# Linear attention of layer 0 rebuilt on one core: one stream of 16 slots, padded heads, sums of squares on TensorE

## The chip, the cores and the metric

The kernel runs on one core of a Trainium2 chip. Its engines are TensorE (PE, with its weight loads shown apart as PEld), VectorE (DVE), ScalarE (ACT), GpSimd (POOL) and SyncE (SP), which issues the DMAs. Metric is the device time of one execution in microseconds (us), median over runs.

## What is computed

Two transformer layers over x of 4 sequences x 512 tokens x 256 features, all float32. The change lies in the first of four parts, a linear attention with 16 heads of 16 features, of which this is the core (the code works in blocks of 128 tokens, which gives the same sums):

```python
qkvu = layernorm(x) @ W_qkvu.T            # q, k, v, u of 256 features each
q, k = silu(q), silu(k)                   # per head, decay s = slope_rate[head]
for block in blocks:                      # kv: the 16x16 state of a head
    o  = (q * exp(-s*i)) @ kv + ((q @ k.T) * exp(-s*(i-j)) [i>=j]) @ v
    kv = exp(-s*len) * kv + (k * exp(-s*(len-i))).T @ v
o = o * rsqrt(mean(o*o, -1) + 1e-6)       # over all 256 features
x = x + (u * o) @ W_out.T
```

The parts behind it (a gated feed-forward layer with Hadamard-transformed weights, a narrow attention, a wide causal attention, a mixture of experts) are untouched in what they compute.

## The kernel before

One program holds a hand-written instruction list for each engine; semaphores order them. Tokens are cut into 16 tiles of 128, four (t) to a sequence (b). Float32 products run as two passes, so one `matmul` is two MATMUL and two LDWEIGHTS records in the trace; a transpose is one of each.

**Start.** SP loads the weights, and TensorE turns them in 12 groups (`START`, lines 514 to 523; `turn_weights`, line 1392), DVE emptying the even groups (line 761) and ACT the odd ones (line 1136). Between its groups ACT makes the decay tables with 16 exponentials (line 1142), which DVE masks (line 764) before it stages the first sequence (line 773). POOL meanwhile runs the butterflies of the feed-forward weights `wugd` (lines 600 and 601) and scales them (lines 610 and 614); its end is the semaphore `fw_done`.

**Linear attention** is a loop over the four sequences in which nothing of one sequence overlaps the next. TensorE: 8 transposes of the normalised x (line 1412), which ACT empties (line 1155); q and k with features on partitions, 8 products of 512 columns (line 1423, emptied by ACT with Silu, line 1167); then per tile k and v in one product pair (line 1431) and u (line 1435), with tokens on partitions, emptied by ACT (lines 1173 and 1174) and DVE (line 784). DVE multiplies q by its decay (line 775), masks k into two copies, even and odd heads (line 781), and multiplies each tile's k by its decay (line 786). Per tile then: the scores of 16 heads, each with 32x128 weights (line 1446), into banks 0 to 3; DVE multiplies them by the decay table (line 796, four per tile); the values: for each head the 128x128 decayed scores are the weights and 16 columns of v move (line 1473), 16 products per tile; the product with the state (line 1479); the new state k.T @ v (line 1461), which DVE masks (line 811) and folds in (line 820). DVE multiplies the output by u (line 805), ACT squares and sums it from the bank (line 1178). When the four tiles are done, `ou` is turned (line 1485), emptied (line 1182) and multiplied by W_out (line 1490, 8 products of 256 columns), and ACT copies the result to `y0` (line 1185).

**After the loop** come, one behind the other: the root of the mean squares (lines 828 and 1188), the residual on all 16 tiles (line 833), the feed-forward weights turned in 16 groups (`FFN`, line 1399, emptied on lines 840 and 1193), the layer norm of all 16 tiles (lines 717, 720, 737), the staging copy (line 845), and TensorE's first transpose of the feed-forward layer (line 1412). Its products are on lines 1509 and 1517. SP waits for `rms_in` (line 556) before it loads the wide attention's weights.

Of the kernel before, what the change touches and what calls it, by code (L numbers as in the profile page):

```python
# [5 lines left out]
ALU = mybir.AluOpType  # L6
# [6 lines left out]
P = 128  # L13
D = 256
# [60 lines left out]
def two_layers(nc, x_in, slope, W_qkvu, W_out0, SU_ug, SU_dp, Wscale_ug, Wscale_dp, W_up, W_gate, W_down,  # L75
               Wq1, Wk1, Wv1, Wo1, ln_w, ff_ln_w, wq, wk, wv, wo, wg, w1, w3, w2, consts, out):
    ctx = ExitStack()
    with ctx:
# [72 lines left out]
        wqkvuT = first.enter_context(nc.sbuf_tensor("wqkvuT", [P, DC, 4 * D], F32))  # L151
        wout0T = first.enter_context(nc.sbuf_tensor("wout0T", [P, DC, D], F32))
# [8 lines left out]
        qT = early.take(DC, S)  # L161
        qdT = early.take(DC, S)
        kT = early.take(DC, S)
        kTm = early.take(2, DC, S)
        ks = early.take(2, D)
        kd = early.take(TB, D)
        v0 = early.take(TB, D)
        u0 = early.take(TB, D)
        PT0 = late.take(2, H16, P)
        kvs = early.take(DC, P)  # L170
        kvt = ks[:, 1, :].rearrange("p (c e) -> p c e", c=DC)
        ou = early.take(TB, D)
        osq = ks[:, 0, :]
        ouT = kT
        ss = early.take(NT)
        y0 = xn

        def head_of(slot):
# [5 lines left out]
        l0 = {n: sem("l0_" + n) for n in ("stage", "xT_ps", "xT_sb", "qk_ps", "q_sb", "kv_ps", "k_sb", "v_sb", "u_ps",  # L184
                                          "u_sb", "kTm", "kd", "s_ps", "pt", "o_ps", "st_ps", "st", "ou", "sq",
                                          "ouT_ps", "ouT_sb", "y_ps", "y_sb", "chain", "qd")}
# [326 lines left out]

        def start_turns():
            for c in range(DC):
                for blocks, dst in ((range(0, 4), wqkvuT[:, c, 0:512]), (range(4, 8), wqkvuT[:, c, 512:1024]),
                                    (range(8, 10), wout0T[:, c, :]), (range(10, 13), wqkv1T[:, c, :])):
                    yield wnat, c, list(blocks), dst
            for i in range(4):
                yield wo_nat, 0, [i, 4 + i], wo1p[:, i, :]  # L520

        wo_nat = xn_st[:].rearrange("p t d -> p (t d)").rearrange("p (n q) -> p n q", q=P)
# [4 lines left out]
        FFN += [(wugd, k % 2, [16 + k // 2, 20 + k // 2], wdT[:, k, :], su_dp[:, k:k + 1]) for k in range(IC)]  # L527


        @block.sync  # L530
        def _(sync):
# [24 lines left out]
            sync.wait_ge(rms_in, 1)  # L556
# [154 lines left out]

        def dve_norm(v, phase, eps, src=x, dst=xn, rms=False):
# [17 lines left out]
            v.wait_ge(ln_std, phase + 1)  # L730
# [11 lines left out]
        def _(v):  # L742
            dve_norm(v, 0, 1e-5)
# [7 lines left out]
            vch.inc(nc.vector.memset(wo_nat, 0.0))  # L751
            vch.wait(v)
            for blk in range(DC):
                ins = nc.vector.tensor_copy(
                    wo_nat[:, 4 * blk:4 * blk + 4, :].rearrange("p i (g d) -> p i g d", d=32)[:, :, :, 0:HD16],
                    wnat[:, 13 + blk, :].rearrange("p (g i d) -> p i g d", g=KV16, d=HD16))
            ins.then_inc(wo_spread, 1)
            for n, (_src, c, blocks, dst) in enumerate(START):
                if n % 2 == 0:
                    v.wait_ge(wt_ps, n + 1)  # L760
                    nc.vector.tensor_copy(dst, bank[n % 8][:, 0:P * len(blocks)]).then_inc(wt_sb[0], 1)
# [5 lines left out]
            v.wait_ge(wt_ps, len(START))  # L767

            ch = Count(l0["chain"], 2)
            with v.Fori(0, B) as b:  # L770
                ch.n = 0
                v.wait_ge(l0["xT_ps"], b * DC + 1)
                nc.vector.tensor_copy(xn_st[:], xn[:, bass.ts(b, TB), :]).then_inc(l0["stage"], 1)
                v.wait_ge(l0["q_sb"], b * 4 + 2)
                nc.vector.tensor_tensor(qdT.rearrange("p c (t i) -> p c t i", t=TB),
                                        qT.rearrange("p c (t i) -> p c t i", t=TB),
                                        QD.unsqueeze(2).to_broadcast([P, DC, TB, P]), ALU.mult).then_inc(l0["qd"], 1)
                v.wait_ge(l0["q_sb"], b * 4 + 4)
                par = const("parity")
                for e in range(2):  # L780
                    nc.vector.tensor_scalar(kTm[:, e, :, :], kT, par[:, e:e + 1], None, ALU.mult).then_inc(l0["kTm"], 1)
                for t in range(TB):
                    v.wait_ge(l0["u_ps"], b * TB + t + 1)
                    nc.vector.tensor_copy(u0[:, t, :], bank[(7, 1)[t % 2]][:, 0:D]).then_inc(l0["u_sb"], 1)
                    v.wait_ge(l0["k_sb"], b * TB + t + 1)
                    nc.vector.tensor_tensor(kd[:, t, :].rearrange("p (h d) -> p h d", h=H16),
                                            ks[:, t % 2, :].rearrange("p (h d) -> p h d", h=H16),
                                            KD.unsqueeze(2).to_broadcast([P, H16, HD16]),
                                            ALU.mult).then_inc(l0["kd"], 1)

                def decay(t):
                    for g in range(4):
                        v.wait_ge(l0["s_ps"], b * 16 + 4 * t + g + 1)
                        if g == 0 and t >= 2:
                            v.wait_ge(l0["o_ps"], b * TB + t - 1)
                        nc.vector.tensor_tensor(PT0[:, t % 2, 4 * g:4 * g + 4, :],
                                                bank[g][:].rearrange("p (h i) -> p h i", h=4),
                                                DT[:, 4 * g:4 * g + 4, :], ALU.mult).then_inc(l0["pt"], 1)

                decay(0)  # L800
                for t in range(TB):
                    if t + 1 < TB:
                        decay(t + 1)
                    v.wait_ge(l0["o_ps"], b * TB + t + 1)
                    nc.vector.tensor_tensor(ou[:, t, :], bank[4 + t % 2][:, 0:D], u0[:, t, :],
                                            ALU.mult).then_inc(l0["ou"], 1)
                    if t < TB - 1:
                        v.wait_ge(l0["st_ps"], b * 3 + t + 1)
                        into = kvs if t == 0 else kvt
                        a, _b = mid("block")  # L810
                        kv_ins = nc.vector.tensor_tensor(into[:], bank[6][:, 0:D].rearrange("p (c e) -> p c e", c=DC),
                                                         con[:, None, a:_b].to_broadcast([P, DC, P]), ALU.mult)
                        if t == 0:
                            kv_ins.then_inc(l0["st"], 1)
                        else:
                            ch.inc(kv_ins)
# [309 lines left out]
        def _(act):  # L1126
# [36 lines left out]
            with act.Fori(0, B) as b:  # L1163
# [4 lines left out]
                for t in range(TB):  # L1168
                    act.wait_ge(l0["kv_ps"], b * TB + t + 1)
                    if t >= 2:  # L1170
                        act.wait_ge(l0["kd"], b * TB + t - 1)
# [676 lines left out]
```

## Time and profile before

| | us |
|---|---|
| median of 3 runs | 2391.54 (2389.66 to 2395.81) |
| the profiled execution | 2396.13 |
| its span | 2394.2 |
| linear attention, first transpose to last output copy | 40.9 to 350.4 |
| from there to the first transpose of the feed-forward layer | 350.4 to 376.9 |
| mean granted TensorE clock of the span | 0.906 of 2.4 GHz |

How to read it: an engine's busy time adds the durations of its instructions; a matmul's duration overlaps that of its neighbours, so the pace of a row of matmuls is the distance of their starts. The granted clock is 1.00 at 2.4 GHz and 0.50 at 1.2 GHz. In the timeline a row merges instructions of one line that follow each other: start, time from the first start to the last end, count, and in brackets how long the engine was idle before and what released it.

### The profile page before, as it was taken

How to read it: one execution, taken by the hardware profiler on the slowest of the kernel's cores; microseconds unless marked ns; L12 is line 12 of the kernel's file. 1: busy time of each engine (PE TensorE's matmuls, PEld its weight loads, DVE VectorE, ACT ScalarE, POOL GpSimd, SP SyncE). 2: the span in 40 equal slices, each digit the busy share in tenths (PEclk: the TensorE clock that was granted, in tenths of full speed). 3: DMA queues.
4: the chain of work that ended last, by engine and by line, in shares of the span. 5: the costliest groups of instructions: out<-in, count | busy, mean ns of one | idle time of the engine just before them, and what ended most of it. 6: DMA issues, size and time to landing. Idle time of an engine off the chain costs nothing.

```text
span 2394.2 us, 36552 instructions
## 1 busy us (share of the span) xinstructions
PE 2030.8 (85%) x10710; PEld 1287.3 (54%) x10710; DVE 1255.0 (52%) x3206; ACT 1041.2 (43%) x2677; POOL 905.6 (38%) x1013
## 2 busy tenths in 40 slices
PE   3889987996687775599999999999999997689995
PEld 2767774554333332366666666666666664555553
DVE  5542233114576675666666666666666666632222
ACT  3012211111454553366565556656565664234442
POOL 4970000000121200244444444444444444268885
PEclk8577668998699998799999999999999999599998
DMA  4000010000000101000000000000000000835556
GB/s 133 1 0 0 0 33 20 0 0 0 0 1 1 36 1 38 1 1 0 0 0 0 0 0 0 0 0 0 0 0 0 0 0 1 283 55 82 83 84 156
DMA packets 61330, 60.47 MB, mean 25 GB/s; under 512 B 13136, under 2 KB 58320, under 8 KB 61264
## 3 DMA queue, kind: packets, MB, share of 16 engines
q0 software_dynamic: 15360, 20.98, 5.5%
q1 hardware_dynamic: 45904, 38.65, 5.0%
q8 instruction: 36, 0.59, 0.1%
q14 instruction: 30, 0.25, 0.0%
HBM read 40.48 MB, written 19.14 MB: 25 GB/s over the span
## 4 chain that ended last, share of the span: by engine, by line
PE 64%; DVE 12%; issue 10%; ACT 7%; POOL 3%; DMA 1%; SPq 1%; ACTq 0%; DVEq 0%; POOLq 0%
PE banks L1549 7%; PE banks L1572 7%; PE banks L1581 6%; PE banks L1509 5%; PE banks L1560 5%; PE banks L1473 4%; PE banks L1591 4%; PE banks L1771 2%; PE banks L1645 2%; PE banks L1517 2%; PE banks L1603 2%; ACT wide_x L1271 2%; PE banks L1620 2%; POOL wdT L692 2%; ACT wugT L1285 2%
## 5 line engine op out<-in xcount | busy, mean ns | idle before, releaser
L900 DVE TENSOR_REDUCE con<-banks 128x1 f32<-128x256 f32 (+3 forms) x512 | 250.0, 488 | 147.7 <-PE banks L1551 141.0
L1549 PE MATMUL banks<-wide_k,wide_q 128*128 128x512 f32 (+3 forms) x1024 | 300.5, 376 | 0.5 <-ACT wide_k L1222 0.5
L624 POOL TENSOR_TENSOR wugT<-wugT,con 128x512 f32<-128x512 f32 (+1 forms) x256 | 237.6, 934 | 134.9 <-DVE con L890 134.3
L1549 PEld LDWEIGHTS banks<-wide_k,wide_q 128*128 128x128 f32 x1024 | 159.3, 190 | 132.3 <-issue 86.2
L1572 PE MATMUL banks<-attn 128*64 128x256 f32 x1280 | 208.5, 404 | 1.0 <-ACT attn L1250 1.0
L1591 PE MATMUL banks<-late,xnT 128*128 (+1 forms) x512 | 197.2, 508 | 9.8 <-DVE xn L916 6.3
L932 DVE TENSOR_REDUCE con<-banks 128x2 f32<-128x1024 f32 x128 | 154.7, 1214 | 68.0 <-PE banks L1633 67.0
L635 POOL TENSOR_TENSOR attn<-attn 128x320 f32<-128x320 f32 x128 | 110.9, 866 | 200.2 <-DVE attn L878 200.2
L1235 ACT ACTIVATE wugT<-banks,con 128x512 f32<-128x512 f32 (+1 forms) x256 | 161.1, 631 | 58.3 <-DVE con L900 55.0
L1581 PE MATMUL banks<-late,attn 128*128 (+1 forms) x512 | 141.7, 399 | 28.0 <-DVE attn L883 25.8
L1771 PE MATMUL banks<-w,late 128*128 x320 | 156.1, 610 | 2.6 <-issue 1.6
L643 POOL MEMSET narrow_x<- 128x2560 f32 x1 | 2.2, 2231 | 399.3 <-DVE x L853 399.3
L922 DVE TENSOR_TENSOR wide_x<-attn,wide_x 128x256 fp32r<-128x256 f32 (+1 forms) x256 | 110.8, 473 | 61.6 <-ACT wide_x L1271 61.6
L706 POOL DMA_INDIRECT y_rows<-xnT,scatter_at x80 | 127.0, 1587 | 34.4 <-issue 22.2
L1560 PE MATMUL banks<-con,wugT 128*128 128x128 f32 x896 | 136.8, 275 | 0.0
L1112 DVE TENSOR_TENSOR late<-late,banks 128x256 f32<-128x256 f32 x80 | 33.7, 421 | 195.5 <-ACT late L1377 168.0
L1250 ACT ACTIVATE attn<-banks 128x512 f32<-128x512 f32 x160 | 95.3, 596 | 92.0 <-PE banks L1560 90.2
L1603 PE MATMUL banks<-ident_r,wide_x 128*128 128x128 f32 x768 | 112.1, 256 | 25.6 <-DVE wide_x L922 22.0
L911 DVE COPY attn<-banks 128x512 f32<-128x512 f32 x160 | 110.0, 688 | 38.4 <-PE banks L1560 38.3
L624 POOL TENSOR_TENSOR wdT<-wdT,con 128x256 f32<-128x256 f32 x128 | 78.4, 613 | 124.5 <-DVE con L890 121.3
L1551 PE MATMUL banks<-causal,ident_h 128*128 128x128 bf16 x512 | 118.1, 231 | 0.0
L1509 PE MATMUL banks<-xnT,wugT 128*128 128x512 f32 x256 | 115.6, 614 | 2.9 <-ACT xnT L1155 2.9
(276 smaller groups left out, 4118.1 us busy)
## 6 DMA issues: line engine op xcount, KB each, us to landing
w<-in_L_ffn_w_dram SPq DMA_DIRECT2D x32, 256.0 KB, 6.3
late<-in_L_ffn_w_dram SPq DMA_DIRECT2D x16, 256.0 KB, 6.4
y_rows<-wqkv1T SPq DMA_DIRECT2D x1, 2176.0 KB, 7.9
x<-in_L_attn_x_dram SPq DMA_DIRECT2D x4, 512.0 KB, 8.8
late<-in_L_ffn_wq_dram SPq DMA_DIRECT2D x2, 1024.0 KB, 7.3
late<-in_L_ffn_wo_dram SPq DMA_DIRECT2D x1, 2048.0 KB, 9.7
h_rows<-wugT SPq DMA_DIRECT2D x1, 2048.0 KB, 7.6
y_rows<-x SPq DMA_DIRECT2D x1, 2048.0 KB, 13.8
```

The source lines that it names most:

```text
L624: nc.gpsimd.tensor_tensor(p, p, rinv[:, m:m + 1].to_broadcast([P, n]), ALU.mult).then_inc(at.sem["norm"], 1)
L900: nc.vector.tensor_reduce(negmax[:, a:a + 1], bank[at.sbank(a)][:, 0:P * at.keys(at.row_of(a))], AX, ALU.max, negate=True).then_inc(at.sem ...
L932: nc.vector.tensor_reduce(n_max[:, s % 4, j // 4, j % 4, :], banks[1 + pair % 2][:].rearrange("p (e n) -> p e n", e=2), AX, ALU.max, negat ...
L1235: nc.scalar.activation(at.prob(m)[:, 0:n], bank[at.sbank(m)][:, 0:n], ACT.Exp, bias=negmax[:, m:m + 1], accum_out=rowsum[:, m:m + 1]).then ...
L1509: ins = nc.tensor.matmul(bank[2 + 2 * (k % 2) + j][:], wugT[:, c, INTER * j + P * k:INTER * j + P * k + P], xnT[:, c, :], start=(c == 0), ...
L1549: nc.tensor.matmul(sbank[:, 0:keys], wide_q[:, side, i, qcols], wide_k[:, side, w, 0:keys], start=(w == 0), stop=False)
L1560: ins = nc.tensor.transpose(bank[PTBANK[a % 2]][:, P * i:P * i + P], at.prob(4 * q + i)[:, P * k:P * k + P], ident)
L1572: ins = nc.tensor.matmul(bank[OBANK][HD64 * e:HD64 * e + HD64, 0:D], wide_v[:, side, k, :], pT.rearrange("p (c e n) -> p e c n", e=2, n=P) ...
L1581: ins = nc.tensor.matmul(bank[YBANK][:, 0:D], at.onT[:, a % ring, P * c:P * c + P], w_out(n, c), start=(c == 0), stop=(c == chunks - 1))
L1591: ins = nc.tensor.matmul(bank[YBANK][:, 0:QKV], xnT[:, c, P * a:P * a + P], w_qkv(n, c), start=(c == 0), stop=(c == DC - 1))
L1603: ins = nc.tensor.transpose(bank[MBANK][:, P * h:P * h + P].bitcast(F32R), src[:, t % 2, z + P * h:z + P * h + P], ident_r[:])
L1771: ins = nc.tensor.matmul(bank[j % 2], m_xT[:, j % 2, c, :], w13[:, bass.ds(e, 1), c, :, :].rearrange("p e i d -> p (e i d)"), start=(c == ...
```

## The change

The four sequences become one unrolled stream of 16 slots, one for each tile (`LIN`). Slot s of each engine holds that tile's values, gate, state and squares, the scores of tile s+1 and the output product of tile s-1. Into three places of each slot (`beside`) the projections of the next sequence are dealt out (`LIN_NEXT`), in the last sequence the 16 groups of feed-forward weights (`FFN`, kinds "w"). These side products and the outputs y share banks 5 and 6 in turn; scores keep banks 0 to 3, the values have bank 4 alone, the new state bank 7.

- The values change sides: v, padded from 16 to 32 features per head, is the weights (128x32) and the 128 columns of decayed scores move, four heads at a time to the four groups of 32 partitions of one bank. The output has features on partitions (4 groups of 128, half of them zeros), so `ou` needs no transposes, and the products with the state are four of 128 columns instead of two.
- u comes with features on partitions too, padded: 4 x 2 products of 512 columns a sequence (`wuS`) for 4 x 2 of 256. W_out is padded likewise (`wout0S`): 4 products of 256 columns a tile for 2.
- The mean square: ACT squares the whole bank into `osq`, and four products with a column of ones as the moving operand sum it into column 256 of the bank of y. ACT copies y and that column.
- k's two masked copies are written by ACT (Silu with the mask as scale) instead of DVE. The staging copy `xn_st` of each sequence goes; x is transposed from `xn`.
- The root, residual, statistics and layer norm run per sequence inside the next sequence's slots (`mean_square`, `residual`, `normalised` on DVE; `rms_root`, `norm_root` on ACT); for the last sequence behind slot 15. SP's wait for `rms_in` becomes one for all four.
- At the start, 16 groups are turned instead of 12 (38 transposes for 34), DVE clears and fills the padded places.

```diff
-        wqkvuT = first.enter_context(nc.sbuf_tensor("wqkvuT", [P, DC, 4 * D], F32))
-        wout0T = first.enter_context(nc.sbuf_tensor("wout0T", [P, DC, D], F32))
+        wqkvT = first.enter_context(nc.sbuf_tensor("wqkvT", [P, DC, 3 * D], F32))
+        wuS = first.enter_context(nc.sbuf_tensor("wuS", [P, DC, H16, 32], F32))
+        wout0S = first.enter_context(nc.sbuf_tensor("wout0S", [P, 4, D], F32))
...
+        turned_bufs = [Region(wugT[:].rearrange("p c n -> p (c n)")), early]
+        qT = [r.take(DC, S) for r in turned_bufs]
+        qdT = [r.take(DC, S) for r in turned_bufs]
+        uT = [r.take(4, S) for r in turned_bufs]
+        kTm = [Region(wdT[:].rearrange("p k d -> p (k d)")).take(2, DC, S), early.take(2, DC, S)]
         ks = early.take(2, D)
+        ou = early.take(2, 4, P)
+        osq = early.take(2, 4, P)
...
+        LIN_FIRST = [("x", 0), ("x", 1), ("q", 0), ("q", 1), ("k", 0), ("k", 1), ("kv", 0), ("u", 0), ("u", 1), ("u", 2), ("u", 3),
+                     ("kv", 1), ("kv", 2), ("kv", 3)]
+        LIN_NEXT = (((("x", 0), ("x", 1)), (("q", 0),), (("q", 1),)), ((("k", 0),), (("k", 1),), (("kv", 0),)),
+                    ((("u", 0),), (("u", 1),), (("kv", 1),)), ((("u", 2),), (("u", 3),), (("kv", 2), ("kv", 3))))
+        LIN = B * TB
+        LIN_BANKS, LIN_O, LIN_STATE = (5, 6), 4, 7
+        def beside(slot, place):
+            b, t = divmod(slot, TB)
+            if b + 1 < B:
+                return [(kind, b + 1, i) for kind, i in LIN_NEXT[t][place]]
+            return [("w", 0, 4 * t + i) for i in ((0,), (1,), (2, 3))[place]]
...
+            sync.wait_ge(rms_in, B)
...
+            vch.inc(nc.vector.memset(wo_nat, 0.0))
+            vch.inc(nc.vector.memset(wo0_nat, 0.0))
+            vch.inc(nc.vector.memset(wuS[:], 0.0))
...
+            nc.vector.memset(v0, 0.0)
+            nc.vector.memset(kvs, 0.0).then_inc(wo_spread, 1)
...
+            def gated(s):
+                b, t = divmod(s, TB)
+                v.wait_ge(l0["o_ps"], s + 1)
+                v.wait_ge(l0["u_sb"], 4 * b + 4)
+                if s >= 2:
+                    v.wait_ge(l0["y_ps"], s - 1)
+                nc.vector.tensor_tensor(ou[:, s % 2], bank[LIN_O].rearrange("p (r i) -> p r i", r=4),
+                                        uT[b % 2][:, :, P * t:P * t + P], ALU.mult).then_inc(l0["ou"], 1)
...
+                else:
+                    vch.inc(nc.vector.tensor_tensor(kvt.rearrange("p (c m) d -> p c (m d)", c=DC), ps, mask, ALU.mult))
+                    vch.wait(v)
+                    v.wait_ge(l0["o_ps"], s + 1)
+                    for c in range(DC):
+                        old = kvs[:, 8 * c:8 * c + 8, 0:HD16]
+                        ins = nc.vector.scalar_tensor_tensor(old, old, BD[:, c:c + 1], kvt[:, 8 * c:8 * c + 8, :], ALU.mult, ALU.add)
+                    ins.then_inc(l0["st"], 1)
...
+            decay(0)
+            decayed_q(0)
+            for t in range(TB):
+                decayed_k(0, t)
+            for s in range(LIN):
+                b, t = divmod(s, TB)
+                if s + 1 < LIN:
+                    decay(s + 1)
+                gated(s)
+                if t < TB - 1:
+                    state(s)
+                for part in range(3):
+                    for kind, n, i in beside(s, part):
+                        if kind == "kv":
+                            decayed_k(n, i)
+                        elif kind == "w" and i % 2 == 0:
...
+                if t == 1 and b + 1 < B:
+                    decayed_q(b + 1)
+                if b >= 1 and t >= 1:
+                    (mean_square, residual, normalised)[t - 1](b - 1)
+            for phase in (mean_square, residual, normalised):
...
+                nc.scalar.activation(osq[:, s % 2].rearrange("p r i -> p (r i)"), bank[LIN_O], ACT.Square).then_inc(l0["sq"], 1)
+            def lin_out(s):
+                at = bank[lin_bank("y", 0, s)]
+                act.wait_ge(l0["y_ps"], s + 1)
+                nc.scalar.activation(y0[:, s, :], at[:, 0:D], ACT.Copy)
+                nc.scalar.activation(ss[:, s:s + 1], at[:, D:D + 1], ACT.Copy).then_inc(l0["y_sb"], 1)
...
+            def lin_values(s):
+                b, t = divmod(s, TB)
+                o = bank[LIN_O]
+                if s >= 1:
+                    pe.wait_ge(l0["ou"], s)
+                    pe.wait_ge(l0["sq"], s)
+                if t >= 1:
+                    pe.wait_ge(l0["st"], 3 * b + t)
+                    pe.wait_ge(l0["qd"], b + 1)
                     for r in range(4):
+                        nc.tensor.matmul(o[:, P * r:P * r + P], kvs[:, 4 * r:4 * r + 4, :].rearrange("p g d -> p (g d)"),
+                                         qdT[b % 2][:, r // 2, P * t:P * t + P], start=(r == 0), stop=False, skip_group_check=True)
+                pe.wait_ge(l0["v_sb"], TB * b + t + 1)
+                for r in range(4):
+                    for g in range(4):
+                        if r == 0:
+                            pe.wait_ge(l0["pt"], 4 * s + g + 1)
+                        ins = nc.tensor.matmul(o[32 * g:32 * g + 32, P * r:P * r + P], v0[:, t, 4 * r + g, :],
+                                               PT0[:, s % 2, 4 * g + r, :], start=(t == 0 and r == 0), stop=(r == 3),
+                                               skip_group_check=True)
+                ins.then_inc(l0["o_ps"], 1)
+            def new_state(s):
+                b, t = divmod(s, TB)
+                pe.wait_ge(l0["kd"], TB * b + t + 1)
+                if s >= 1:
+                    pe.wait_ge(l0["st"], 3 * b + t)
                 for c in range(DC):
+                    ins = nc.tensor.matmul(bank[LIN_STATE][:, P * c:P * c + P], kd[:, t, P * c:P * c + P],
+                                           v0[:, t, 8 * c:8 * c + 8, 0:HD16], start=True, stop=True)
+                ins.then_inc(l0["st_ps"], 1)
+            def lin_out(s):
+                n = lin_bank("y", 0, s)
+                at = empty(n)
+                pe.wait_ge(l0["sq"], s + 1)
+                for r in range(4):
+                    nc.tensor.matmul(at[:, D:D + 1], osq[:, s % 2, r, :], const("ramp")[:, 0:1], start=(r == 0), stop=(r == 3))
+                for r in range(4):
+                    ins = nc.tensor.matmul(at[:, 0:D], ou[:, s % 2, r, :], wout0S[:, r, :], start=(r == 0), stop=(r == 3))
+                ins.then_inc(l0["y_ps"], 1)
+                emptied[n] = l0["y_sb"], s + 1
+            early_uses, late_uses = LIN_FIRST[:6], LIN_FIRST[6:]
+            lin_side([(kind, 0, i) for kind, i in early_uses])
+            scores(0)
+            lin_side([(kind, 0, i) for kind, i in late_uses])
+            for s in range(LIN):
+                if s + 1 < LIN:
+                    scores(s + 1)
+                lin_side(beside(s, 0))
+                lin_values(s)
+                lin_side(beside(s, 1))
+                if s % TB < TB - 1:
+                    new_state(s)
+                if s >= 1:
+                    lin_out(s - 1)
+                lin_side(beside(s, 2))
+            lin_out(LIN - 1)
```

## Rows read from the trace of the kernel before

**Rows 1.** The page: engine totals, and TensorE's clock in 40 slices of the span.

```profile
PE 2030.8 (85%) x10710; PEld 1287.3 (54%) x10710; DVE 1255.0 (52%) x3206; ACT 1041.2 (43%) x2677; POOL 905.6 (38%) x1013
...
PEclk8577668998699998799999999999999999599998
```

**Rows 2.** Windows: PE, PEld, DVE, ACT, POOL busy, clock, DMA share, GB/s.

```profile
40.90:125.70 84.80, 71.80 (x360) 57.31 (x360) 41.51 (x39) 11.85 (x27) 83.39 (x37) 0.64 0.00 1
...
203.80:278.60 74.80, 68.16 (x360) 55.00 (x360) 20.24 (x39) 12.84 (x28) 0.00 (x0) 0.68 0.00 0
278.60:350.40 71.80, 64.95 (x361) 51.88 (x361) 19.54 (x38) 13.04 (x30) 0.00 (x0) 0.71 0.00 0
350.40:376.90 26.50, 7.39 (x49) 6.76 (x49) 24.02 (x77) 7.43 (x12) 0.00 (x0) 0.65 0.48 119
```

**Rows 3.** Windows of 4 us, PE alone: busy (matmuls), granted clock, DMA.

```profile
60.00:64.00 4.00, 4.00 (x14) 1.00 0.02 4
76.00:80.00 4.00, 4.00 (x20) 0.50 0.00 0
600.00:604.00 4.00, 2.53 (x9) 0.50 0.00 0
692.00:696.00 4.00, 3.02 (x28) 1.00 0.00 0
```

**Rows 4.** Timeline of PE, third sequence of the linear attention.

```profile
206.13 7.13 PE L1423 MATMUL banks<-xnT,wqkvuT 128*128 128x512 f32 x16 [1.23 <-ACT xnT L1155]
...
214.82 1.03 PE L1435 MATMUL banks<-wqkvuT,xnT 128*128 128x256 f32 x4
...
224.19 1.17 PE L1446 MATMUL banks<-early 32*128 32x128 f32 x32 [0.61 <-DVE early L784]
225.30 0.71 PE L1461 MATMUL banks<-early 128*128 128x128 f32 x4
226.10 3.11 PE L1446 MATMUL banks<-early 32*128 32x128 f32 x32
...
252.99 7.01 PE L1473 MATMUL banks<-early,late 128*128 128x16 f32 x32
```

**Rows 5.** Timeline of PE in the narrow attention, values with 128x32 weights.

```profile
691.60 1.06 PE L1645 MATMUL banks<-wugT,attn 128*32 128x512 f32 x8
692.60 0.54 PE L1654 MATMUL banks<-ident_r,narrow_mx 128*128 128x128 f32 x4
```

**Rows 6.** Timeline of all engines, behind the last sequence.

```profile
350.38 3.71 PE L1399 MATMUL banks<-con,early 128*128 128x128 f32 x32 [0.78 <-ACT xn L1185]
...
352.18 6.43 DVE L833 SCALAR_TENSOR_TENSOR x<-xn,rstd,x 128x256 f32<-128x256 f32 x16
...
363.13 5.31 DVE L717 BATCH_NORM_STATS2 st<-x 128x6 f32<-128x256 f32 x16
...
376.88 1.97 PE L1412 MATMUL banks<-con,xn_st 128*128 128x128 f32 x8 [13.75 <-DVE xn_st L845]
```

**Rows 7.** Timeline of all engines, start of the first sequence.

```profile
34.60 0.63 ACT L1136 ACTIVATE wo1p<-banks 128x256 f32<-128x256 f32 x2
34.72 3.85 DVE L764 TENSOR_TENSOR late<-late,con 128x2048 f32<-128x2048 f32 x1 [6.31 <-ACT early L1147]
...
40.92 1.33 PE L1412 MATMUL banks<-con,xn_st 128*128 128x128 f32 x5 [12.75 <-DVE xn_st L773]
43.58 9.24 PE L1423 MATMUL banks<-xnT,wqkvuT 128*128 128x512 f32 x16 [0.69 <-ACT xnT L1155]
```

**Rows 8.** Lines of DVE: ns min/median/max, first and last start; POOL's last work.

```profile
L786 DVE TENSOR_TENSOR early<-early x16: 416/1324/2233, 59.0 to 298.9; 128x256 f32<-128x256 f32 x16
L796 DVE TENSOR_TENSOR late<-banks,late x64: 675/681/693, 68.6 to 329.7; 128x512 f32<-128x512 f32 x64
L820 DVE SCALAR_TENSOR_TENSOR early<-early x16: 344/352/2475, 93.1 to 334.0; 128x128 f32<-128x128 f32 x16
166.64 2.33 POOL L614 TENSOR_SCALAR early<-early,ws_dp 128x1024 f32<-128x1024 f32 x2
```

More of the change, by code:

```diff
@@ L764, in _ @@
             vch.inc(nc.vector.tensor_tensor(DT, DT, con[:, None, a:_b].to_broadcast([P, H16, P]), ALU.mult))
-            vch.wait(v)
[L767 to L776, printed above, removed]
-                                        QD.unsqueeze(2).to_broadcast([P, DC, TB, P]), ALU.mult).then_inc(l0["qd"], 1)
[L778 to L816, printed above, removed]
-                            ch.wait(v, b)
-                            v.wait_ge(l0["st"], b * 5 + 2 * t - 1)
-                            for c in range(DC):
-                                nc.vector.scalar_tensor_tensor(kvs[:, c, :], kvs[:, c, :], BD[:, c:c + 1], kvt[:, c, :],
-                                                               ALU.mult, ALU.add).then_inc(l0["st"], 1)
@@ new lines, in normalised @@
+            def normalised(b):
+                rows = slice(TB * b, TB * b + TB)
+                v.wait_ge(ln_std, b + 2)
+                vch.inc(nc.vector.reciprocal(rstd[:, rows], std[:, rows]))
+                vch.wait(v)
+                for t in range(TB * b, TB * b + TB):
+                    nc.vector.tensor_scalar(xn[:, t, :], x[:, t, :], mv[:, t, 0:1], rstd[:, t:t + 1],
+                                            ALU.subtract, ALU.mult).then_inc(xn_all, 1)
+            decay(0)
+            decayed_q(0)
@@ L1133, in start_weights @@
                 for n in turns:
[L1134 removed]
+                    _src, _c, _blocks, copies = START[n]
                     act.wait_ge(wt_ps, n + 1)
[L1136 removed]
+                    for dst, part in copies:
+                        ins = nc.scalar.activation(dst, part(bank[n % 8]), ACT.Copy)
+                    ins.then_inc(wt_sb[1], 1)
             start_weights(range(1, 9, 2))
@@ new lines, in scores @@
+            def scores(s):
+                b, t = divmod(s, TB)
+                cols = slice(P * t, P * t + P)
+                pe.wait_ge(l0["q_sb"], 2 * b + 2)
+                pe.wait_ge(l0["k_sb"], 2 * b + 2)
+                for r in range(4):
+                    for g in range(4):
+                        if r == 0 and s >= 1:
+                            pe.wait_ge(l0["pt"], 4 * (s - 1) + g + 1)
+                        rows = slice(32 * g, 32 * g + 32)
+                        ins = nc.tensor.matmul(bank[g][:, P * r:P * r + P], kTm[b % 2][rows, r % 2, r // 2, cols],
+                                               qT[b % 2][rows, r // 2, cols], start=True, stop=True)
+                        if r == 3:
+                            ins.then_inc(l0["s_ps"], 1)
```

364 lines of the change are left out of this document (201 added, 163 removed).

## The prediction

> **What bounds the kernel now.** I read the page first: TensorE is busy for 85% of the span, and its clock in the second to sixth of the 40 slices (60 to 360 us) is 5, 7, 7, 6 and 6 tenths, the longest low run there is [rows 1]. The change touches only what lies before the feed-forward layer, so I cut that stretch with the windows view: the linear attention takes 309.5 us (40.9 to 350.4), and 26.5 us of norms and weight turning follow before TensorE's next stage [rows 2]. In the sequences TensorE is busy 85 to 91% of the time, DVE 27 to 49%, ACT 14 to 18%. So TensorE bounds it, but at a mean clock of 0.64 to 0.71. The 4 us windows say where the clock goes: while projections run it is granted 1.00, while the values run (line 1473) 0.50, with the engine shown busy all the time in both [rows 3]. The timeline of one sequence gives the reason to suspect: the values are 32 passes of only 16 moving columns, 7.01 us a tile, 0.22 us a pass, and that is the load of 128 weight columns, not the product [rows 4]. Four of them a sequence are 28 us of some 75, and they leave the clock low for the transposes and the first half of the output product behind them. Behind the last sequence TensorE works 7.4 of 26.5 us while DVE walks through 16 tiles three times [rows 2, 6].
>
> **The change, part by part.** I sum TensorE's work of one sequence at full clock, since a bound engine sets the end, and add waits afterwards. A product is two passes.
> - Projections: q and k 16 passes of 512 columns, u 16 (8 of them new, from the padding), k with v 16: 48 passes. Sixteen took 7.13 us [rows 4], 0.44 each with the last one's tail taken off: 21.1 us. Eight transposes at 3.71 / 32 = 0.116 [rows 6]: 0.9.
> - Scores, unchanged: 32 passes in 1.17 us at full clock [rows 4], four times: 4.7.
> - Values, new form: 32 passes of 128 columns with 128x32 weights. No row has this shape. Lower bound: eight passes of 512 columns with 128x32 weights in the narrow attention start at 691.60 and the next line at 692.60, 1.00 us for 4096 columns, and ours are 32 x 128, also 4096 [rows 5]. Upper bound: no overlap between the four column groups, a quarter of 0.44 per pass, 3.5 us. I take 1.17, the scores' price: the same count, the same 128 columns, the same four-way split. Four tiles: 4.7, where 28 were.
> - State: 3 tiles of 8 passes of 128 columns at 0.116: 2.8. New state: four passes take 0.80 us until the next line starts (225.30 to 226.10) [rows 4], three times: 2.4.
> - Output: 8 passes of 256 columns a tile at half of 0.44: 7.0 a sequence, twice that of before; the 8 transposes of `ou` and their two copies go.
> - Squares over the column of ones: 8 passes a tile whose price is the weight load. Line 1473 has it with 16 columns at half clock, 0.22; half of that is 0.11, 3.5 us a sequence. This is the one part that puts work on the bound engine which ACT did for nothing before (its squares summed on line 1178, not on DVE): some 14 us in all; what it saves on ACT is covered.
>
> Sum: 21.1 + 0.9 + 4.7 + 4.7 + 2.8 + 2.4 + 7.0 + 3.5 = 47.1 us a sequence. Four are 188.4, and the feed-forward weights (48 transposes at 0.116, now in the last sequence's slots) 5.6: 194 us of TensorE work for 309.5 plus the turning.
>
> **Start.** Before, the first transpose waited until 40.9 for DVE, which had masked the decay table (line 764) and then staged x. Now it waits for ACT's copies of the start weights only: four behind the exponentials instead of two, at 0.63 for two from 34.60: 35.9 [rows 7]. To the first projection 2.7 us as before (40.92 to 43.58): 38.5. Sixteen passes 9.2, partly at half clock [rows 7]: 47.8. ACT's last Silu copies hold the scores back by some 1.5, scores 1.2, then 32 passes 14.1, and DVE's four k decays, slow beside POOL at up to 2.2 us [rows 8], perhaps 0.5: slot 0 starts at 65. The clearing of v's padding on DVE (twice the 1024 elements of a clearing it already makes) ends near 42, before the first v is copied. The 4 more transposes at the start are under ACT's exponentials.
>
> **The slots.** Of the 194 us, 23.2 lie before slot 0 (21.1, 0.9, one scores). The rest is 170.8. To that I add three things. The switches between full, row-split and column-split products: four passes of line 1461 between two runs of scores took 0.80 where 4 x 0.116 is 0.47, so 0.33 for two switches [rows 4]; four a slot (64, 10.6 us), less those already in the new state's price (24, 4.0): 6.6 us. Waits for DVE and ACT: 10 us, a choice. A few microseconds of half clock: 3. Together 190.4, so slot 15 ends at 255.4.
>
> What covers DVE: a slot asks of it 2.5 (four of line 796 at under 0.7) for the decays, 0.7 for the gate, about 1.1 for the state, 0.4 for k, and a quarter of the residual and norm, 1.4 [rows 6, 8]: 6.1, under TensorE's 11.8, in the last sequence some 7 beside TensorE's 7.4. The order on DVE matters there: in slot 14 the whole residual of the sequence before stands ahead of the decays that TensorE's next scores wait for; that is where part of the 10 us goes. ACT had 13 us a sequence [rows 2]; with the wider squares, the second copy of k and the roots it stays at some 20. Bank 4 is single: values s+1 wait for gate (0.7) and square (0.6) of s. Between them TensorE has the new state, the output product, a side product and the next scores, at least 4 us, so this wait costs nothing while DVE is punctual; if DVE is late by more than 3 us it is paid in full. A squaring late on ACT also holds the side copies behind it.
>
> **Behind slot 15**: the copy of y 1.0, mean square and root 1.8 (as 350.4 to 352.2), residual a quarter of 6.43, statistics a quarter of 5.31, the layer norm as much [rows 6], aggregates and second root 2, staging copy 0.7: 9.7. The feed-forward layer's first transpose starts at 265.1, where it was 376.88. Everything later shifts as it is; SP's loads for the wide attention start later but are wanted hundreds of us later.
>
> **The number.** 376.9 less 265.1 is 112 us; from the profiled execution's 2396.1 that leaves 2284. The median of the runs lies 4.6 under that execution, so I forecast 2280.
>
> **A rule against it.** The profile shows half clock during values with the engine busy [rows 3], and later in the narrow attention 0.50 at a busy share of 2.53 in 4 and 1.00 at 3.02 in 4 [rows 3]. [...] The Trainium skill, TensorE: Matmul & The Clock Gate, Part 4, says that transpose-mode products do not count as busy for the clock. If that decided, the last sequence, in which 48 transposes replace the projections, would be the place where the clock falls; it is the third rival. Line 1399 of before speaks against it here: 32 transposes at 0.116 each, full speed, right behind dense products [rows 6].
>
> **Rivals.**
> 1. DVE becomes the bound while POOL runs (until 169) [rows 8]. Then lines with two SBUF inputs take 2.2 to 2.5 instead of 0.4: k decays 8.9 a sequence, state folds 8.8, q decay 3.1, the residual up to 9; with decays 9.9, gates 2.8, norms and the rest 5.5 that is 48 us against TensorE's 47, in the same order-bound chain. For it: the medians of rows 8. Against: only slots 0 to 8 lie there and not all folds collide. It costs the misfit of two equal loads, some 27 us beyond my 10: 2307. Chance 0.13.
> 2. The four column groups do not overlap: 3.5 instead of 1.17 a tile, 16 x 2.3 = 37: 2317. Against: rows 5. Chance 0.03.
> 3. The last sequence's slots run at half clock: 23.9 + 5.6 = 29.5 us of work twice: 2310. Chance 0.10.
> 4. Slower than before: the clock stays at 0.50 through the whole stream, because the squares' one-column passes, the scores and the gaps of a wait in each slot thin it out, and once low it does not come back, as in rows 3 at 600 us. Then 170.8 is paid twice: 2280 + 171 = 2451. It decides from 112 / 171, two thirds of the slot work at half clock; below that the kernel is still faster. Against: in the third sequence the clock came up within the projections each time, and every slot but the last four holds 5 us of 512-column passes. Chance 0.04.
>
> That the change does nothing has no mechanism: the 26.5 us behind the loop shrink by themselves.
>
> **Chances and range.** My forecast has 0.70, its own range 2262 (waits 5 less, switches hidden, values at 1.0) to 2300. The likely rivals reach 2317, and two of them together 2330. So 2260 to 2330. What a measurement can tell from no change is about 0.3%, 7 us; all cases but the fourth are far below that: faster 0.95, slower 0.04, same 0.01.
>
> **What would show it.** First transpose of the feed-forward layer near 265; slot 0 near 65; values rows of 32 passes near 1.2 us; output column passes near 0.11; clock 0.9 or more between 65 and 255; DVE's k decays still 2.2 under POOL and 0.4 after. Wrong would be: TensorE idle of more than 20 us in the slots, ended by DVE (rival 1), values rows of 3 us (rival 2), clock 0.5 behind about 220 us (rival 3) or throughout (rival 4).

## The result, and the profile after

The changed kernel takes 2286.11 us (median of 4 runs, 2284.21 to 2292.86) where the kernel before takes 2390.72 in the runs beside it: ratio 0.9563, 95% interval 0.9539 to 0.9588. Its profiled execution has a span of 2285.3 us, 108.9 less. Forecast was 2280, range 2260 to 2330.

The page: engine totals and the clock in 40 slices of 57 us (answers to [rows 1]).

```profile
PE 1951.5 (85%) x10922; PEld 1195.0 (52%) x10922; DVE 1262.5 (55%) x3207; ACT 1056.8 (46%) x2712; POOL 905.2 (40%) x1013
...
PEclk9989899967999978999999999999999997799998
```

TensorE's share has not changed, but the low run of the clock at the second to sixth slices is gone. What took 309.5 + 26.5 us between 40.9 and 376.9 now ends at 270.32. The windows view of the new stretches, with columns as in [rows 2]: slots before the stand, slots 5 to 7, slots 8 to 11, the last sequence, the tail.

```profile
65.30:136.80 71.50, 71.50 (x682) 47.44 (x682) 50.85 (x53) 22.65 (x49) 70.32 (x32) 1.00 0.00 1
136.80:166.60 29.80, 19.23 (x122) 13.73 (x121) 26.04 (x29) 7.23 (x14) 28.06 (x24) 0.78 0.00 1
166.60:219.90 53.30, 53.30 (x495) 35.11 (x495) 26.41 (x62) 22.27 (x45) 2.71 (x3) 0.99 0.01 1
219.90:262.40 42.50, 33.64 (x315) 27.58 (x313) 21.12 (x51) 10.07 (x24) 0.00 (x0) 0.88 0.01 1
262.40:270.30 7.90, 0.00 (x0) 0.00 (x0) 6.23 (x21) 2.14 (x5) 0.00 (x0) 0.75 0.78 199
```

In the first and third stretch TensorE has no gap at all, and a clock of 1.00 and 0.99. The loss sits in the second and fourth. Below, a stand is time in which TensorE waits, and cold passes are those that run at half clock. One undisturbed slot in PE's timeline of the changed kernel (answers to [rows 4, 5]):

```profile
130.05 1.17 PE L1606 MATMUL banks<-early 32*128 32x128 f32 x32
131.16 1.98 PE L1591 MATMUL banks<-xnT,wuS 128*128 128x512 f32 x4
132.98 1.05 PE L1622 MATMUL banks<-early,late 128*128 128x128 f32 x8
133.96 1.08 PE L1629 MATMUL banks<-late 128*32 128x128 f32 x32
134.97 1.98 PE L1591 MATMUL banks<-xnT,wuS 128*128 128x512 f32 x4
136.79 0.61 PE L1641 MATMUL banks<-late 128*128 128x128 f32 x4
139.29 1.14 PE L1651 MATMUL banks<-con,early 128*128 128x1 f32 x8 [1.89 <-ACT wugT L1276]
...
161.09 1.86 PE L1651 MATMUL banks<-con,early 128*128 128x1 f32 x8 [8.68 <-ACT wugT L1276]
162.81 3.76 PE L1653 MATMUL banks<-wout0S,early 128*128 128x256 f32 x8
```

From start to start: scores 1.11, a side product 1.82, the product with the state 0.98, values (line 1629) 1.01 for 32 passes where line 1473 took 6.9. Then two stands, of 1.9 and 8.7 us, and behind the long one everything at half clock: the squares 1.7 instead of 0.8, the output 3.6 instead of 1.8. DVE in the same stretch:

```profile
136.22 2.29 DVE L880 TENSOR_SCALAR early<-early 128x4 f32<-128x4 f32 x1
...
148.41 9.82 DVE L889 SCALAR_TENSOR_TENSOR x<-xn,rstd,x 128x256 f32<-128x256 f32 x4
...
160.22 2.47 DVE L827 TENSOR_TENSOR late<-banks,late 128x512 f32<-128x512 f32 x4
```

The four residuals of the first sequence take 2.46 us each beside POOL, and the decays of the next scores stand behind them. ACT stands too, for the second root, with u's copy behind it:

```profile
146.33 1.28 ACT L1316 ACT_TABLE_LOAD   x1
160.34 0.20 ACT L1316 ACTIVATE std<-var 128x4 f32<-128x4 f32 x1 [12.73 <-DVE var L897]
160.46 0.58 ACT L1276 ACTIVATE wugT<-banks 128x512 f32<-128x512 f32 x1
```

In the last sequence TensorE waits before the output product of each slot:

```profile
222.93 1.87 PE L1651 MATMUL banks<-con,early 128*128 128x1 f32 x8 [2.75 <-DVE wugT L927]
...
236.07 1.05 PE L1651 MATMUL banks<-con,early 128*128 128x1 f32 x8 [1.83 <-DVE wugT L927]
...
245.91 1.05 PE L1651 MATMUL banks<-con,early 128*128 128x1 f32 x8 [1.56 <-DVE wdT L927]
...
254.47 1.05 PE L1651 MATMUL banks<-con,early 128*128 128x1 f32 x8 [2.15 <-DVE wdT L927]
...
270.32 1.97 PE L1548 MATMUL banks<-con,xn_st 128*128 128x128 f32 x8 [7.96 <-DVE xn_st L939]
```

Releaser is DVE's copy of a weight group (line 927), which lies in the bank that y needs; DVE's list has it behind gate and state.

### The profile page after: what moved, and what is told of

Same layout as the page of the kernel before. It is cut to its first block, busy times and chain, and to the rows that moved or that the text cites. A ratio compares the mean times of both kernels' runs of the same rounds, so it can differ in the third digit from the quotient of the medians.

```text
span 2285.3 us, 36870 instructions
## 1 busy us (share of the span) xinstructions
PE 1951.5 (85%) x10922; PEld 1195.0 (52%) x10922; DVE 1262.5 (55%) x3207; ACT 1056.8 (46%) x2712; POOL 905.2 (40%) x1013
## 4 chain that ended last, share of the span: by engine, by line
PE 65%; DVE 12%; issue 11%; ACT 7%; POOL 3%; DMA 1%; SPq 1%; ACTq 0%; DVEq 0%; POOLq 0%
PE banks L1725 8%; PE banks L1748 7%; PE banks L1757 6%; PE banks L1685 5%; PE banks L1736 5%; PE banks L1767 4%; PE banks L1947 3%; PE banks L1821 3%; PE banks L1693 2%; PE banks L1591 2%; PE banks L1779 2%; PE banks L1796 2%; ACT wide_x L1407 2%; POOL wdT L729 2%; PE banks L1653 2%
## 5 line engine op out<-in xcount | busy, mean ns | idle before, releaser
L1206 DVE TENSOR_TENSOR late<-late,banks 128x256 f32<-128x256 f32 x80 | 33.7, 421 | 195.1 <-ACT late L1513 177.3
```

## The experiments

I measure each run by two numbers: its median, and the length of the slots in its profile, from slot 0's first scores pass (65.27 in the changed kernel) to the feed-forward layer's first transpose (270.32): 205.0 us. The start before slot 0 ends between 62.2 and 65.3 us in the profiles, and what follows that transpose takes 2015 to 2020 us; this length leaves both out. The runs below come from three sets, in which the kernel before has medians of 2386.01, 2391.61 and 2387.42, beside 2390.72 for the result above. So two medians of different sets can differ by some 5 us that no edit made, and where median and length disagree I go by the length. Four theories had to be told apart for the 197.1 us from slot 0 to the end of the last output product, of which about 30 are waits and cold passes (the last section but two has that sum): TensorE's own work, the groups' overlap, DVE beside POOL, and the order of the lists.

**What the squares on TensorE cost.** Without the four products, and with them twice:

```diff
                 for r in range(4):
-                    nc.tensor.matmul(at[:, D:D + 1], osq[:, s % 2, r, :], const("ramp")[:, 0:1], start=(r == 0), stop=(r == 3))
```

> The changed kernel without the four products with the column of ones (128 passes over 16 tiles, 0.79 us a tile in its profile); ACT writes a constant in their place, so the mean square is left out of the computation. Theory (TensorE bounds the stream): the stage shortens by nearly all of 16 x 0.8 = 12.6 us, less what falls into waits of the last sequence and of the two stalls under POOL (six tiles or so), so 8 to 12 us: median 2275 to 2278. Rival (DVE or ACT bound the stream and TensorE's work is filler): under 4 us, median above 2282.

> The changed kernel with the four products with ones issued twice a tile, the second set into the next column. Theory (TensorE bounds the stream): plus 8 to 13 us, median 2294 to 2299. Rival (waits bound it): plus under 4 us. Second question, the clock: one-column passes thin out the dense columns; if they pull the clock down, the stage shows 0.5 in slots where it showed 1.0, and the loss is far above 13 us.

Without: 2273.72 us, slots 63.83 to 255.06, 191.2 us, 13.8 less. Twice: 2304.3 us, slots 221.6 us, 16.5 more. Both are outside the theory's numbers, on the far side from the rival: the stream is TensorE's, and the ones cost more than their 12.6 us. In the changed kernel they take 15.5 us from start to start, 7.3 in the nine tiles at full pace and 8.2 in the seven around the stands and in the last sequence.

The second question has two answers. In the slots with projections the doubled ones left the clock alone: the windows from 64 to 156 us still show 1.00. The last sequence, from slot 12's scores to the end of the last output product, took 55.8 us for 46.0, where five second sets of 0.90 us are 4.5. TensorE's waits there are no longer than before (7.8 for 8.6), but the granted clock is 0.79 for 0.89, and without the ones it is 0.96. Three other runs with the same work in that sequence show 0.83 to 0.92, so how much of this is the one-column passes and how much the place of the waits is not shown.

**The groups of columns.** Values issued group by group:

```diff
-                for r in range(4):
-                    for g in range(4):
+                for g in range(4):
+                    for r in range(4):
```

> The changed kernel with the 16 value products of a tile issued group by group (four in a row to the same 32 columns of the array) instead of in turn over the four groups; same instructions, same sums. Theory (the 1.01 us a tile come from four groups running side by side): without that neighbour overlap a pass costs its 128 columns, 0.107, so 3.4 us a tile, 38 us more in all: median near 2322. Rival (the pace is the issue of 32 short passes, whatever their order): the tile stays at 1.0 to 1.3 us, median within 5 us of 2286.

```profile
64.36 2.46 PE L1629 MATMUL banks<-late 128*32 128x128 f32 x32
66.75 1.98 PE L1591 MATMUL banks<-xnT,wqkvT 128*128 128x512 f32 x4
```

2.39 us a tile for 1.01: the order matters, so the four groups do run side by side. The single records of the first tile, sorted by their even distances into four rows of eight, say why it is not 3.4. The eight passes of a group start 0.109 us apart, their full price, but the next group's first pass starts 0.467 us after the first of the group before, when that one has three passes still to start. So passes of one group do not overlap, and two neighbouring groups still do. The median is 2295.45 and the slots 213.8, only 8.7 more where 16 x 1.38 = 22 were added. The rest came out of the stands and the cold passes behind them: TensorE's waits in the slots are 10.7 us in place of 19.2 (4.5 for 10.6 before u's copies), since a slower TensorE reaches those places later. Both stated numbers missed; the direction is the theory's.

**POOL and the norms.** First the norms of sequence 1 moved behind POOL's end, then POOL's work left out.

```diff
-                if b >= 1 and t >= 1:
-                    (mean_square, residual, normalised)[t - 1](b - 1)
+                for b_, k in PHASE_AT.get(s, []):
+                    (mean_square, residual, normalised)[k](b_)
```

with `PHASE_AT` giving (sequence, step) for each slot: (0,0) in 8, (0,1) in 9, (0,2) and (1,0) in 10, (1,1) in 11, (1,2) in 12, the third sequence as it was; ACT's roots follow the same table.

> The changed kernel with root, residual, statistics and layer norm of the first sequence moved from slots 5 to 7 to slots 8 to 10, behind the end of POOL's butterflies, those of the second to slots 10 to 12. Theory (in slots 5 and 6 DVE's instructions with two SBUF inputs run against POOL at 2.2 to 2.5 us, and TensorE stands 1.9 and 8.7 us and then runs cold): 14 to 18 us less, median 2268 to 2272, residual lines 0.4 us each. Rival (the order of ACT's roots is what stops TensorE, wherever they stand): under 5 us less, the same stall in slot 9.

> The changed kernel with POOL's butterflies and scaling of the feed-forward weights left out (they are turned as loaded), so nothing shares DVE's second SBUF port. It measures all that POOL costs this stage. Theory: the stalls of slots 5 and 6 vanish as in the run with the norms moved, and DVE's k and q decays fall to 0.4 and 1.1 us; TensorE had cover for those, so 15 to 20 us less, median 2266 to 2271, within 3 us of the run with the norms moved. Rival (DVE's slow decays cost too): more than 5 us below that run.

Norms moved: 2279.28 us, slots 195.1, 9.9 less. POOL idle: 2273.02, slots 188.4, 16.6 less. Neither median is in its theory's range, and the second is 6.3 us under the first, which by the stated number is the rival's sign that DVE's slow decays cost too. The lengths up to slot 12 decide it. The lines of the run with the norms moved: DVE's residuals (min/median/max in ns), and TensorE's new stand in slot 12.

```profile
L890 DVE SCALAR_TENSOR_TENSOR x<-xn,rstd,x x16: 475/480/485, 176.2 to 252.6; 128x256 f32<-128x256 f32 x16
...
207.79 1.87 PE L1653 MATMUL banks<-con,early 128*128 128x1 f32 x8 [5.10 <-DVE wugT L928]
```

Up to slot 12's scores the run with the norms moved is 15.3 us shorter (135.8 for 151.1), the size expected, and equal within 0.5 us to the run with POOL idle (135.3). So DVE's slow k and q decays under POOL cost TensorE nothing, and the norms' steps beside POOL cost all of it: the four residuals (9.82 us in a row before the stand of 8.7) and, ahead of the stand of 1.9, the mean square, for which ACT's root waited. No run moved one of these steps alone. Behind slot 12 this run gave back 5.4 us, a stand of 5.10 for 2.75 and more cold passes. I had also shifted the second sequence's residual from slot 10 to 11, in front of the first slot of weights; with those norms back at slots 9 to 11 and the copy's order changed too (both mends, below) the stand is 1.8.

**Is it ACT's order?** The roots put a slot later, behind the square:

```diff
                 squared(s)
+                if b >= 1 and t >= 2:
+                    (rms_root, norm_root)[t - 2](b - 1)
                 lin_side(beside(s, 1))
...
-                if b >= 1 and t in (1, 2):
-                    (rms_root, norm_root)[t - 1](b - 1)
```

> The changed kernel with ACT's two roots moved from the end of slots t=1 and t=2 to slots t=2 and t=3, behind the square, where DVE has already passed what they wait for; DVE's list unchanged. Theory (DVE itself is late under POOL: its decays stand behind the residual, so freeing ACT helps only until TensorE needs the next scores): 3 to 6 us less than the changed kernel. Rival (the whole 8.7 us stand is ACT waiting in order, with u's copies held behind it): 12 us or more less, as with the norms moved out of POOL's reach.

```profile
141.36 3.78 PE L1574 MATMUL banks<-wqkvT,xnT 128*128 128x512 f32 x4 [4.25 <-ACT wugT L1276]
...
165.44 5.90 PE L1574 MATMUL banks<-wqkvT,xnT 128*128 128x512 f32 x8 [10.43 <-ACT wugT L1276]
```

2297.24 us, slots 212.5: 7.5 longer, where both theories had less. ACT no longer stood at the root, it stood at the square before it (its wait for the gate, line 852, was 13.6 us), since the gate too is behind the residual on DVE; the root's table loads came on top, in front of u's copies. So ACT, which the view names as releaser, only passed on a wait of its own, and DVE's list was the cause. The theory's reason holds; its number is refuted, in sign too.

**The order of the last sequence**, and both mends together (with sequence 2's norms back at slots 9 to 11):

```diff
                 if s + 1 < LIN:
                     decay(s + 1)
+                if b + 1 == B:
+                    weight_copy(4 * t)
                 gated(s)
...
-                for part in range(3):
+                for part in range(3) if b + 1 < B else (1, 2):
```

> The changed kernel; in the last sequence DVE copies the slot's first group of feed-forward weights before the gate and the state instead of behind them, so the bank that the output product needs is free in time. Theory (the waits of 2.7, 1.8, 1.6 and 2.2 us for that copy, and the cold passes behind the first and last, are an order fault of DVE's list): from slot 0 to the feed-forward layer's first transpose 8 to 12 us less than the 205.0 of the changed kernel, median 2275 to 2279. Rival (another wait, ACT's copy or the state, ends at the same point): under 3 us less.

> Both mends together, and the second sequence's norms kept at slots 9 to 11 (in the run with the norms moved they had gone to 10 to 12, where their residual in slot 11 made a new stand of 5.1 us in slot 12). Theory: stage from slot 0 to the feed-forward layer 205.0 less 16 less 9 = 180, median 2261 to 2266. Rival (each mend moves the stand on): 190 or more, median above 2271.

Order alone: slots 198.4, 6.6 less, median 2282.41. Length and median both miss the forecast: of the four waits of 2.75, 1.83, 1.56 and 2.15 us two vanish, and 1.8 and 1.5 stay where DVE comes to the copy late from its norm phases. Both mends: 2264.19 us, in the forecast range, and slots 183.3 where 180 was forecast; the ratio to the kernel before is 0.9467 (0.9442 to 0.9492).

**Half the passes for the squares**, on top of these:

```diff
-                    nc.tensor.matmul(at[:, D:D + 1], osq[:, s % 2, r, :], const("ramp")[:, 0:1], start=(r == 0), stop=(r == 3))
+                    nc.tensor.matmul(at[:, D:D + 2], osq[:, s % 2, r, :], ones_r[:], start=(r == 0), stop=(r == 3))
```

with `osq` and `ones_r` (two columns) declared as fp32r.

> The version with both mends, and the squares and the column of ones kept as fp32r, so that each of the four products is one pass instead of two. Theory (in a stream that TensorE bounds, half of these passes is half of their 0.8 us a tile): from slot 0 to the feed-forward layer's first transpose 183.3 less 16 x 0.4 = 177, median 5 to 7 us under that version's 2264. Rival (the four weight loads of 128 float32 columns cost the same in fp32r, or the waits of the last sequence swallow it): under 2 us less.

```profile
77.59 0.58 PE L1661 MATMUL banks<-ones_r,osq 128*128 128x2 f32 x4
78.04 1.97 PE L1663 MATMUL banks<-wout0S,early 128*128 128x256 f32 x8
```

0.45 us a tile for 0.81, and slots 177.3 for the 177 expected. The median is 2259.55 us, 4.6 under that of both mends where 5 to 7 were forecast, but in another set of runs; the ratio to the kernel before is 0.9465 (0.9438 to 0.9493) against 0.9467. So the gain of 6.0 us is shown by the slots alone, in one profile each, and not by the times of the whole kernel.

**The old form of the values**, in the kernel before:

```diff
-                    for slot in range(H16):
...
+                        ins = nc.tensor.matmul(o[:, 0:D], PT0[:, t % 2, slot, :], v0[:, t, :], start=True,
...
```

> The kernel before, with one product of 256 moving columns a tile for the values (the first head's scores against all of v) instead of 16 products of 16 columns: 15 of 16 heads' values are left out. It tells what the old form of the values cost, and whether it was this form that held the clock at half. Theory (sparse columns lower the clock of everything around them): the 16 x 7.0 us fall to 16 x 0.5 to 0.9, about 100 us, and the scores, state and output products around them, 2.1 against 1.2 us and so on, run at full clock in most tiles, another 10 to 20 us: linear attention 309.5 less 110 to 120, median 2270 to 2280. Rival (the clock follows the waits between the sequences' stages, not the form): 95 to 102 us less, scores still near 2.1 us a tile, median 2289 to 2296.

```profile
190.72 0.91 PE L1471 MATMUL banks<-early,late 128*128 128x256 f32 x2
193.82 1.23 PE L1461 MATMUL banks<-early 128*128 128x128 f32 x4 [2.19 <-DVE early L811]
194.98 2.09 PE L1446 MATMUL banks<-early 32*128 32x128 f32 x32
197.00 1.13 PE L1471 MATMUL banks<-early,late 128*128 128x256 f32 x2
197.96 0.61 PE L1477 MATMUL banks<-early 128*128 128x128 f32 x4
201.03 0.99 PE L1461 MATMUL banks<-early 128*128 128x128 f32 x4 [2.46 <-DVE early L820]
```

2312.96 us: 74 less than the kernel before in the same runs (2387.42), and the linear attention ends at 271.15 instead of 350.38. Neither number was met. With nearly all of the values' work gone, TensorE waits longer for DVE's mask and fold (2.19 and 2.46 us in the lines above, where the same sequence of the kernel before has 0.85 and 1.60), and scores still run at 2.09 us, half clock, in two of the four tiles. The long values had been hiding these waits. The mean clock of the linear attention rose from 0.68 to 0.79 and no further, so the sparse form was not all that held it down; the low pieces left lie in and behind the stretches with waits. The changed kernel, with all its values computed, is 27 us faster than this one. So at least that much of the gain cannot come from a shorter product for the values; how it splits between the stream and the norms inside it was not measured.

## Why the prediction was right

**The bound.** TensorE's work sets the stream. Taking the squares' products out moved the slots by 13.8 us and doubling them by 16.5, for 12.6 priced; halving their passes moved them by 6.0, for 16 x 0.36 = 5.8. Slower values moved them by 8.7 of 22, the rest fell into the stands. And 2 of the 4 windows of the slots above have no gap. That step held.

**The pieces.** From start to start, against the forecast: four projection passes 1.82 (1.76); scores 1.11 (1.17); values 1.01 (1.17, bounds 1.0 and 3.5: the lower bound was the truth); products with the state 0.98 (0.93); new state 0.45 (0.80); output 1.81 (1.76); squares 0.81 (0.88). Up to slot 12's scores the stream with nothing in the way takes 135.3 us (POOL idle). The same stretch, which holds eleven output products and not twelve, was priced at 138.7 without the switches between splits and at 143.6 with them.

The term for these switches, 6.6 us, was not wanted on top, but switches do cost. Three projection passes in front of a full-width product, and three in front of scores:

```profile
135.51 1.45 PE L1591 MATMUL banks<-xnT,wuS 128*128 128x512 f32 x3
...
71.10 1.45 PE L1591 MATMUL banks<-xnT,wqkvT 128*128 128x512 f32 x3
```

The next line starts 1.28 us later in the first case (136.79) and 1.38 in the second (72.48). The pass ahead of the first three, right behind the values, takes 0.54 (134.97 to 135.51), and the one ahead of the other three, behind a full-width product, 0.43 (70.67 to 71.10). So a change between full width and a split costs about 0.1 us on each of its two sides. With the other starts of a slot read in the same way, its four changes cost some 0.7 us. The distances above hold that already, and so did 1.17 for scores and for values; the forecast counted it again. The new state now stands between full-width products and has no switch, which is why it takes 0.45 where it took 0.80 between two runs of scores [rows 4].

**The waits.** Here the forecast was too low: 10 us of waits and 3 of half clock, a choice, as the text says. Slots 0 to 11 took 151.1 us, 15.8 over the undisturbed 135.3. The last sequence took 46.0 (216.38 to 262.36); it holds five output products, so the like of it was priced at 32.1 and not at 29.5, and at the distances above, with some 7 us for its 48 transposes, its work is about 32: 14 of waits and cold passes. In all 197.1 for 190.4: some 167 us of work where 177.4 were priced with the switches, and 30 of waits and cold passes where 13 were. The hit is thus in part luck: an error of 17 us and one of 10 the other way. TensorE stood idle for 19.2 us in the slots, just under the 20 that the text names as the sign of rival 1.

**DVE beside POOL** was the first rival at a chance of 0.13 and 27 us. It came true in one place: 15 to 16 us, by two runs that agree. My covering argument compared averages (DVE's 6.1 us a slot under TensorE's 11.8) and named the wrong slot, 14, for the residual before the decays; in slot 6 it is the same order with residuals of 2.46. The sum of rival 1 was right for the residual and wrong for the rest: the slow k and q decays and state folds cost nothing that these runs show.

**The clock.** Rival 3, half clock in the last sequence, came in small: 0.88 in its window. The low pieces stand behind the waits of 2.75 and 2.15 us; between 232 and 256 us, with transposes and the waits of 1.83 and 1.56, the clock is 1.00, and four transposes take 0.49 there. The rule of the Trainium skill (TensorE: Matmul & The Clock Gate, Part 4) that transposes do not count as busy in the same way is neither shown nor refuted by this trace, since every low piece has a wait in front of it. Rival 4, half clock throughout, did not happen; nor did rival 2, since the groups overlap.

**Start and tail.** Slot 0 at 65.27 (65 forecast; it is 62.2 to 63.8 in the profiles of the other versions, so a hit to 0.3 us is luck), tail from the last output pass 8.0 (9.7), first transpose of the feed-forward layer 270.32 (265.1). 106.6 of the 108.9 us are gone by there; the other 2.3 are within the 5 us by which the rest differs between profiles.

## What to carry to other kernels

When a product has few moving columns, its weights are its price: at full clock a pass with 128x128 weights took 0.11 us here whether 1, 2 or 128 columns moved (line 1651, line 1661 of the fp32r version, and line 1622). Swap the sides, and issue neighbours to different column groups. When a loop of separate stages becomes one stream, price each in-order list with its longest item, not with its average: one block of slow instructions ahead of what the bound engine needs next is paid nearly in full (9.82 us of residuals, a stand of 8.7), and again in the cold passes behind it. Read a wait's releaser one step further back, to what the releaser itself waited for.

## What I had not expected of the hardware

- Thirty-two passes with 128x32 weights and 128 columns take 1.01 us in turn over four column groups, and 2.39 us group by group: 0.109 a pass within a group, with two neighbouring groups side by side for over half of the time.
- One-column passes, 16 in a row (1.84 us) in every slot, left the clock at 1.00 in the slots with projections; in the last sequence it was 0.79 with them, 0.89 with 8 and 0.96 with none, one profile each. In a stand of 8.7 us the clock fell to 0.50 and stayed there for some 6 us of work behind it (0.50 at 160 to 164 us, 0.57 at 164 to 168, then 1.00).
- A change between full-width and split weights costs about 0.1 us on each of its sides.
- A residual with two SBUF inputs takes 0.48 us alone and 2.46 beside POOL; even the mean square of 4 elements a partition (line 880) took 2.3 there, and 0.17 behind POOL's end.
- Four products of 128 weight columns take 0.45 us in fp32r and 0.81 in float32: a pass costs about the same (0.11 and 0.10), and their number halves.
